# State-space branch of a graph network: front in bands of 512 columns, both channel halves scanned in one stage, skip term as a diagonal product, gate on GpSimd

## The reference, cut to what matters

```python
xc = sum((xp[k:k + n] * conv_w[:, k] for k in range(K))) + conv_b      # K = 4
xc = silu(xc)
dbc = xc @ x_proj_w.T                                                  # 16 + 16 + 16 columns
dt = softplus(dbc[:, :16] @ dt_proj_w.T + dt_proj_b)
Bm, Cm = dbc[:, 16:32], dbc[:, 32:]
A = -exp(A_log)
dA = exp(dt[:, :, None] * A)
dBx = (dt * xc)[:, :, None] * Bm[:, None, :]
h = dA_t * h + dBx_t ; y_t = h @ C_t                                   # scan over the nodes
y = (y + xc * D_param) * silu(z)
return y @ out_proj_w.T
```

## Time and profile before

| | us |
|---|---|
| median of 3 runs (7149.9 to 7175.03) | 7159.76 |
| the profiled execution, its own time | 7162.67 |
| its span, first to last instruction | 7161.0 |
| busy of the whole span: PE | 4387.5 (61%) |
| DVE | 3985.8 (56%) |
| POOL | 2280.8 (32%) |
| ACT | 1870.2 (26%) |
| mean granted TensorE clock | 0.786 of 2.4 GHz |
| `mamba`, from its first transfer at 2388.69 to the first of the next stage at 2970.24 | 581.55 |

### The profile page before, as it was taken

How to read it: one execution, slowest core, us unless ns; L and a number is a source line. 1 busy time by engine, 2 the same in 40 slices (tenths; PEclk the granted TensorE clock), 3 DMA queues, 4 the chain that set the end, 5 groups by cost and what they waited for, 6 DMA issues and landing times. The chain is left out here.

```text
span 7161.0 us, 83841 instructions
## 1 busy us (share of the span) xinstructions
PE 4387.5 (61%) x18940; PEld 2318.0 (32%) x18941; DVE 3985.8 (56%) x6280; ACT 1870.2 (26%) x2810; POOL 2280.8 (32%) x2170
## 2 busy tenths in 40 slices
PE   4888476234997266389756677556776444550387
PEld 2454375111443032274323333223333122220123
DVE  7987376698996599454322333222332112227997
ACT  1475111013884322244201111001111001110254
POOL 0000000500000065210266666566665666660000
PEclk8999687667998588699877888677887666665797
DMA  1471675434664277405555566555666444454444
GB/s 33 154 236 46 215 251 178 147 115 140 181 180 132 94 272 256 160 29 198 183 160 173 185 202 205 158 160 179 201 200 191 134 136 133 133 140 117 138 135 119
DMA packets 465303, 1145.77 MB, mean 160 GB/s; under 512 B 62936, under 2 KB 253935, under 8 KB 452553
## 3 DMA queue, kind: packets, MB, share of 16 engines
q1 hardware_dynamic: 293397, 550.53, 24.0%
q0 software_dynamic: 134816, 447.33, 21.1%
q10 hardware_dynamic: 36996, 146.80, 5.6%
HBM read 886.09 MB, written 261.55 MB: 160 GB/s over the span
## 5 line engine op out<-in xcount | busy, mean ns | idle before, releaser
L2681 POOL DMA_INDIRECT rel1s_rows<-rel_table,rel1s_at x640 | 625.8, 978 | 367.8 <-issue 283.7
L2681 POOL DMA_INDIRECT rel2s_rows<-rel_table,rel2s_at x640 | 615.4, 962 | 382.9 <-issue 221.4
L2681 POOL DMA_INDIRECT rel0s_rows<-rel_table,rel0s_at x640 | 623.3, 974 | 343.4 <-issue 288.6
L2883 PE MATMUL rel2s_acc<-rel2s_rows,rel2s_hot 128*128 x732 | 401.2, 558 | 490.7 <-issue 323.3
L2125 POOL TENSOR_TENSOR mamb_st<-mam_u,mamb_bc 128x1600 f32<-128x1600 f32 x64 | 230.0, 3593 | 1139.4 <-DMA mamb_bc<-dbc 1139.4
L1676 PE MATMUL gatx_acc<-gatx_w,gatx_feat 128*65 128x400 f32 x1600 | 540.6, 500 | 26.0 <-DVE gatx_w L1568 26.0
L2883 PE MATMUL rel1s_acc<-rel1s_rows,rel1s_hot 128*128 x732 | 329.2, 466 | 242.2 <-issue 164.3
L2883 PE MATMUL rel0s_acc<-rel0s_rows,rel0s_hot 128*128 x732 | 319.5, 455 | 250.0 <-issue 176.0
L1568 DVE SCALAR_TENSOR_TENSOR gatx_w<-gatx_w,gatx_adj 128x1600 f32<-128x1600 f32 x200 | 363.3, 1818 | 0.5 <-ACT gatx_w L1624 0.5
L1676 PE MATMUL latx_acc<-latx_w,latx_feat 128*65 128x400 f32 x800 | 291.7, 509 | 101.3 <-DVE latx_w L1568 101.3
L1415 DVE CUSTOM_DVE_ANT_0 gatm_junk<-gatm_srow,gatm_gone 128x3125 bf16<-128x3125 f32 x100 | 335.7, 3412 | 27.5 <-DMA gatm_srow<-gat_scores 23.2
(11 more groups left out here) (612 smaller groups left out, 9156.1 us busy)
## 6 DMA issues: line engine op xcount, KB each, us to landing
mamb_bc<-dbc SPq DMA_DIRECT2D x128, 800.0 KB, 5.9
agg_strip<-strips SPq DMA_DIRECT2D x100, 800.0 KB, 5.8
gatx_adj<-adj SPq DMA_DIRECT2D x200, 400.0 KB, 3.1
adj<-adj_counts SPq DMA_DIRECT2D x25, 1600.0 KB, 7.1
latx_adj<-adj SPq DMA_DIRECT2D x100, 400.0 KB, 3.1
rel_table<-rel0p_prod POOLq DMA_DIRECT2D x25, 1536.0 KB, 6.3
rel_table<-rel0s_prod ACTq DMA_DIRECT2D x25, 1536.0 KB
rel_table<-rel1s_prod ACTq DMA_DIRECT2D x25, 1536.0 KB
```

The lines of the kernel that those rows point to most:

```text
L2681: pool.indirect_dma_start(rows[k][:, u, :], None, table, bass.IndirectOffsetOnAxis(ap=at[:, n:n + 1], axis=0)).then_inc(s_in[u], 16)
L2883: one = nc.tensor.matmul(acc[a][:, :], hots[k], most_two[k], start=fresh and k == 0, stop=False)
```

## The change

- **Front.** `mamac`, `mamae`, `mamag` and `mamas` become one stage. It goes through the node axis in seven bands (`BANKS`: six of 512 columns and one of 128). Each band has its own transfer of `raw`, then eight convolution instructions on VectorE that alternate between the channel halves, SiLU, the `dbc` product, its eviction, the `dt` product and two evictions of it, one as it is (Identity) and one as Abs into `u`. ScalarE handles in turn j the SiLU of band j, the `dbc` of band j-1 and the `dt` of band j-2. Exp and Ln follow on both halves in instructions of 3200 columns; the two VectorE instructions of half 0 end the stage, those of half 1 (`later`) are put at the head of VectorE's list in the scan stage.
- **No detour over DRAM for `xsT`.** `conv_x` is gone; `xsT` stays in SBUF. The gate is loaded into `yT` behind the bands' transfers.
- **One scan stage** of 64 steps `(ct, half, n)`. The barrier, the start-up and the end between the channel halves are gone.
- **Skip term.** `acc` is opened by a float32 product of `xsT` with a diagonal matrix `diag` of `D_param` (four matmuls over 1600 columns) in place of the bfloat16 product of zeros.
- **Gate.** After steps 16, 32 and 48 ScalarE copies `acc` into `dt` and GpSimd multiplies it into `yT` (1600 columns, behind its product of the third step of the next group). The last quarter is gated by VectorE straight from `acc`, in four instructions.
- **Output.** The output product is in the same stage and uses the four banks of `dA`; `y_sorted` is stored in two transfers of 12 and 13 node tiles. The first six pairs of tiles need only the first three quarters of `yT`.

The diff, cut to its core (what it removes stands in full in the listing above):

```diff
+        xsT = top.sb("xsT", [P, 2, NP])
+        yT = top.sb("yT", [P, 2, NP])
+        diag = top.sb("diag", [P, 2, P])
...
+            def _(sp):
+                for j, (a, b) in enumerate(BANKS):
+                    sp.dma_start(raw[:, :, K - 1 + a:K - 1 + b], raw_dram.rearrange("k p n -> p k n")[:, :, a:b]).then_inc(s_in[j], 16)
+                sp.dma_start(yT[:, :, :], z_dram.rearrange("k p n -> p k n")).then_inc(s_z, 16)
+                sp.wait_ge(s_dbc, NB)
+                sp.dma_start(dbc_dram, dbc[:, :]).then_inc(s_st, 16)
...
+                for k in range(2):
+                    nc.vector.tensor_scalar(diag[:, k, :], g.ident[:, :], cols[:, 2, k:k + 1], None, ALU.mult)
...
+                for j, (a, b) in enumerate(BANKS):
+                    dve.wait_ge(s_in[j], 16)
+                    for c in range(K):
+                        for k in range(2):
+                            if c == 0:
+                                ins = nc.vector.tensor_scalar(xsT[:, k, a:b], raw[:, k, a:b], cw[:, k, 0:1], None, ALU.mult)
+                            else:
+                                dve.wait_ge(s_v, n - 1)
+                                ins = nc.vector.scalar_tensor_tensor(xsT[:, k, a:b], raw[:, k, a + c:b + c], cw[:, k, c:c + 1],
+                                                                     xsT[:, k, a:b], ALU.mult, ALU.add)
...
+                dve.wait_ge(s_ln, 1)
+                p(nc.vector.scalar_tensor_tensor(dt[:, 0, :], dt[:, 0, :], 0.0, u[:, 0, :], ALU.max, ALU.add))
+                p(nc.vector.tensor_tensor(u[:, 0, :], dt[:, 0, :], xsT[:, 0, :], ALU.mult))
...
+                for j, (a, b) in enumerate(BANKS):
+                    if j >= 2:
+                        pe.wait_ge(s_dbc, j - 1)
                     for k in range(2):
+                        pe.wait_ge(s_silu, 2 * j + k + 1)
+                        last = nc.tensor.matmul(xmm[j % 2][0:R + 2 * S, 0:b - a], xT[:, k, :], xsT[:, k, a:b], start=k == 0, stop=k == 1)
+                    last.then_inc(s_x, 1)
+                    if j:
+                        stepped(j - 1)
...
+                    if j >= 2:
+                        a, b = BANKS[j - 2]
+                        for k in range(2):
+                            m = 2 * (j - 2) + k
+                            act.wait_ge(s_d, m + 1)
+                            nc.scalar.activation(dt[:, k, a:b], dmm[m % 4][:, 0:b - a], ACT.Identity, bias=cols[:, 1, k:k + 1])
+                            nc.scalar.activation(u[:, k, a:b], dmm[m % 4][:, 0:b - a], ACT.Abs, bias=cols[:, 1, k:k + 1]).then_inc(s_dt, 1)
...
+            todo = [(ct, half, n) for ct in range(2) for half in range(2) for n in range(S)]
+            outv = u[:, :, :].rearrange("p k n -> p (k n)").rearrange("p (t d) -> p t d", d=D)
+            whole = HALF // P // 2
...
+                    if q > S and n == 2:
+                        i = q // S - 1
+                        pool.wait_ge(s_copied, i + 1)
+                        at = when(i % 2)
+                        nc.gpsimd.tensor_tensor(yT[:, i // 2, at], yT[:, i // 2, at], dt[:, i // 2, at], ALU.mult).then_inc(s_yT, 1)
...
+                later = Tick(s_later, dve)
+                later(nc.vector.scalar_tensor_tensor(dt[:, 1, :], dt[:, 1, :], 0.0, u[:, 1, :], ALU.max, ALU.add))
+                later(nc.vector.tensor_tensor(u[:, 1, :], dt[:, 1, :], xsT[:, 1, :], ALU.mult))
...
+                dve.wait_ge(s_y, len(todo))
+                for a, b in spans:
+                    nc.vector.tensor_tensor(yT[:, 1, HALF + a:HALF + b], acc[:, a:b], yT[:, 1, HALF + a:HALF + b], ALU.mult).then_inc(s_yT, 1)
...
+                        for a, b in spans:
+                            nc.tensor.matmul(acc[:, a:b], diag[:, ct, :], xsT[:, ct, half * HALF + a:half * HALF + b], start=True, stop=False)
...
+                pe.wait_ge(s_h, len(todo))
+                pe.wait_ge(s_yT, 3)
+                for q, pr in enumerate(pairs):
+                    if q == whole:
+                        pe.wait_ge(s_yT, 3 + len(spans))
+                    if q >= 4:
+                        pe.wait_ge(s_e, q - 3)
+                    for n, t in enumerate(pr):
+                        for k in range(2):
+                            last = nc.tensor.matmul(dA[:, (q % 4) * BANK + n * D:(q % 4) * BANK + (n + 1) * D],
+                                                    yT[:, k, t * P:(t + 1) * P], outT[:, k, :], start=k == 0, stop=k == 1)
```

323 lines of the change are left out of this document (139 added, 184 removed).

## The result

The changed kernel takes 7076.75 us (median, 7070.87 to 7084.35) against 7164.02 in runs of the kernel before on the same chip (7149.9 to 7175.03): a ratio of 0.9876, 95% interval 0.9858 to 0.9893. The forecast was 7074 us (range 7058 to 7098). The profiled execution took 7078.49 us, its span is 7076.8, so 84.2 less than the span before. The state-space branch, counted as before from its first transfer to that of the next stage, takes 2885.20 - 2391.20 = 494.00 us instead of 581.55: 87.6 less. All stages ahead of it and behind it together take 3.3 us more, which no step of the change explains and which is within the scatter of these runs.

A forecast was written before the change was run, and what follows sets the result against it. The prediction took single-engine waits at stage ends as the cost, and VectorE's work as the bound of scan steps. Terms -42.0 + 2.6 - 12.6 + 5.7 - 39.7 = -86.0 us gave 7074 us as a median, range 7058 to 7098.

The forecast's parts named there:

- Front, -42.0: Stretch from the branch's start to the scan stage: 106.0 us before, 64.0 after the change, so 42.0 us less.
- Softplus 11.5: End of the front: Exp on both halves, table loads and Ln on one half, 11.5 us ahead of VectorE's part.
- with hand-overs I take 9.3: Front behind the last convolution: ScalarE's remaining SiLU and evictions, 8.2 us, taken as 9.3 with hand-overs.
- Rival 1: Front: TensorE limits it, at a low clock from the second band on; +7.5 us, total 7081; chance 0.20.
- Start of the scan, +2.6: Scan stage's start: GpSimd's first product waits for VectorE's half 1 softplus; first scan at 10.7 instead of 8.1 us.
- Seam -12.6: Between the channel halves: VectorE's 14.7 us of idling go, a 2.1 us wait for ScalarE comes instead.
- gates +5.7: Three gate products on GpSimd each make VectorE's product by C wait 1.9 us; bounds 0 and 16.4.
- rival 2: Steps: GpSimd's next product gets in first (+10.7), or diagonal products run at low clock (up to +12); 7085 to 7097; chance 0.11.
- Diagonal, 0: Float32 diagonal product, 2.2 us more on TensorE at three seams, hidden by GpSimd's lead: cost 0, upper bound 12 us.
- Tail, -39.7: From the last product by C to the next stage: 74.85 us before, 35.1 after, so 39.7 us less.
- The lock: Scan stage: a VectorE product of two SBUF tensors and a GpSimd product exclude each other, first come, first served.
- Rival 4: Steps 18 to 63: GpSimd's product lies across each product by C, +3.1 us in 46 steps, +142, total 7216; chance 0.03.

The follow-up runs named there:

- 128-row version: Changed kernel with the front's dt product on 128 rows instead of 16, dbc and weights padded with zeros: branch 490.4 us against 494.0.
- long convolution's run: Changed kernel with the convolution's operations over all 3200 columns after every band has landed, the rest still in bands: branch 512.4 us against 494.0.
- four-state-tile version: Changed kernel plus zero-padded 128-row dt product, GpSimd's products held under scans, gates on VectorE, six broadcast and four state tiles: 6627.83 us, ratio 0.9841.

## Why the prediction was right

**Front, -42.0: measured -38.0.** Convolution 35.7, measured 34.7. Softplus 11.5, measured 11.45 (2440.23 to 2451.68). The term that was mis-sized is "with hand-overs I take 9.3": 14.4 in the changed kernel, 8.4 in the four profiles with 128 rows, 8.7 to 16.1 in eight with 16. The tail behind the convolution was reckoned at TensorE's full clock, and the last bands ran at 0.50. Rival 1 had that mechanism but not its size: it let TensorE be slow from the second band on without a break (+7.5), and the lasting fall came in the fifth band (+4.0). The spread over eight kernels, 62.4 to 69.7, takes in the forecast's 64.0 and nearly reaches the rival's 71.5, so it was no either-or but a scatter of the clock.

The Trainium skill ("TensorE: Matmul & The Clock Gate", Why this matters for your kernels) makes the loop nest decide whether products stay warm, by how TensorE is kept busy. The trace of the changed kernel goes against busy time as the whole answer: the clock fell with TensorE busy but for 0.33 us, and stayed up in the 128-row version with 0.96 us of idling before each of the last full bands. The long convolution's run, at 0.99 for 20 us without a gap, agrees with the Trainium skill.

**Start of the scan, +2.6: measured +2.5** (first scan 10.56 us into the stage, 8.07 before; forecast 10.7). It was 10.56 or 10.57 in every version. Counted from the start of `mamba` the first scan came at 78.6 us, where the prediction named 75; the difference is the front's.

**Seam -12.6 and gates +5.7.** Together with the steps themselves: the two blocks of steps took 377.9 us before, and the sum allowed 7.8 on top (2.1 of waiting at the new seam, 5.7 for gates). Measured 382.2, so 4.3. The products by C cost 152.6 - 146.8 = 5.8, as forecast to 0.1, and the run without gates takes 5.9 away. That agreement is in part luck: each gate made one product by C 3.0 to 3.4 us longer than 1.82, not 1.9, so that these took 4.8 to 5.2 us and not the 3 to 4 that the prediction named, and 3.6 us came back in the others. At the first gate it was GpSimd's next product that got in first, as rival 2 had it, though not at its price. What was oversized is the wait at the seam: 0.65 us, and at all three seams 1.2 in all where the two before had 2.7. That wait scatters, 1.6 us in the other profile of the changed kernel and 6.0 in the run without gates.

**Diagonal, 0:** no gain when it is left out.

**Tail, -39.7: measured -41.6** (33.24 us). The output product took 21.80 instead of 24.0, at a granted clock of 0.94. The forecast took only 0.56 off the 24.56 for coming warm, and 2.76 was right: in the kernel before, ScalarE could start on the first pair 3.8 us into the product, on the second 2.7 later, and on each full pair behind it 1.73 later. Behind TensorE's end came 8.54 instead of 8.1. The last gate ran beside the first pairs.

**Sum -86.0: measured -87.6 in the branch, -84.2 in the span.** Two misses, +4.0 in the front and -5.4 in steps and tail, nearly cancel: the hit of the total owes something to luck, as does that of the gates' term. The start, the diagonal and softplus came out as reckoned. The stated chances add up to 1.02, not 1; no term of the sum hangs on that.

**The lock.** The reading of the earlier trace rows, first come, first served between a VectorE product of two SBUF tensors and a GpSimd product, carried the start and the gates. The runs show it from the other side: with GpSimd's products under the scans, the products by C lose what they had above 1.8 to 1.9 us, 2384 ns to 1871 on average. The Trainium skill's rule ("SBUF — State Buffer", Who interferes with whom) is that contention, and the trace agrees.

**Rival 4** did not come, and the argument against it ("the phase is set anew in each step", by the broadcast's landing) was the right one: taking that wait away brought its mechanism, in 27 of the 64 steps, at a mean of 3219 ns. That is below what would have turned this change into a loss (4.2 us over 46 steps, or 2.29 + 86 / 64 = 3.6 over all 64), but it took more than half of the gain in the branch (544.0 against 581.55 before).

The prediction missed something too: it took the mean of 2.29 us for the product by C as given, though 1.82 stood in the earlier trace rows. (2.29 - 1.87) x 64 = 27 us were there before the change and are still there after it. The four-state-tile version gets them.

## What to carry to other kernels

Where two engines exclude each other, the time of one's instruction depends on when the other's starts. Compare the shortest record of a group with its mean, and if they differ, put the other engine's work under something that it does not disturb, with a wait if need be. Before enlarging a ring, ask what sets the phase once its wait is gone: here a transfer's lateness kept GpSimd out of VectorE's way.

Cutting a front into bands gains by letting the engines work side by side; reckon its end at both levels of TensorE's clock.

## What the hardware showed that was not expected

- A larger ring alone cost 55.7 us in 64 steps (382.2 to 437.9), and an added wait with the same ring then won 79.6 (437.9 to 358.3).
- First come, first served is fine-grained: GpSimd's second of two products (7.64 us together, from 2566.79) began some 0.2 us before VectorE's product by C asked at 2571.12, and the latter took 5.00.
- The granted clock in the fronts with 16-row products falls to 0.50 at a place that changes from run to run, and the front with it (62.4 to 69.7 us); with zero-padded 128-row products it was 61.9 to 62.2 in four of four, and TensorE's time for a band's dt product was 1.98 us, the narrow one's at full clock.
- The gathers of a later stage were some 8 ns longer each (955 to 963 ns) in kernels that differ only in the branch. This is open.
